# Replanned order, constant batches on GpSimd behind gates, and bound arithmetic on VectorE, in a graph and FFN layer

## The chip, the cores and the metric

One core of a Trainium2 chip runs the whole kernel. The metric is the device time of one execution in microseconds. Times of the parts come from one profiled execution.

## The reference

N = 3125 nodes of D = 256 features, E = 100,000 edges sorted by their target `dst`, each with a source and a relation (0 or 1).

```python
f = layernorm(x)
S = f[src]
msgs = where(rel == r, relu(relu(S @ W_rel[r].T + b_rel[r]) @ W_rel[r].T + b_rel[r]), ...)   # r = 0, 1
agg = segment_sum(msgs, dst, 3125)
i, f, g, o = split(agg @ W_ih.T + b_ih + b_hh, 4)
c = sigmoid(i) * tanh(g);  hn = sigmoid(o) * tanh(c)
x = x + relu(relu(hn @ W1.T + b1) @ W2.T + b2) @ W3.T + b3
n2 = layernorm(x);  w = n2 @ wr + br                 # one weight a node
sel = the 1561 nodes of largest w (ties to the lower index)
x = x + n2;  x[sel] += (gelu(n2[sel] @ w1 + b1) @ w2 + b2) * w[sel]
```

## The kernel before

The nodes lie in 25 blocks of 128, grouped in seven super-blocks (4, 4, 4, 4, 4, 3, 2 blocks). The messages depend on the source and the relation alone, so the **head** computes them once for each node and relation: for each super-block `s` a layer norm (`ln`, VectorE with a square root on ScalarE), transposes (`featT`), two products with the relation weights (`L1`, `L2`), and on VectorE `add_bias` and `low`, which with ScalarE write a high and a low fp16 half of each message to the tile `late` (`lows(s)` is this pair for all blocks of `s`). SyncE stores them to the table `message_table`. VectorE runs `lows(s)`, then `ln(s + 2)`, then one extra step; TensorE runs `L1(s)`, `featT(s + 1)`, `L2(s)`. TensorE waits for `ln`, and for at most three blocks of `add_bias` behind it.

The edges lie in 782 tiles of 128. The first 424 ("hot") are aggregated by counting: for each tile VectorE makes a mask of keys (`key`, L1723) and, for every four tiles, of rows (`rows`, L1732), TensorE multiplies them into banks (`count`, L1384), ScalarE evicts these counts (L1119), and `dense` (L1397) multiplies counts with the messages. The last 369 tiles ("cold") are gathered by GpSimd from the table, one indirect DMA a tile (L1046), into a ring of eight groups of four; TensorE sums a group with a mask (`visit`, L1416; a "chunk" is the part of a group that falls into one 128-node span), and frees it for GpSimd. GpSimd pauses behind every seventh group until the one before has landed. The tiles' places are predicted from statistics of the edges; **bounds** (`low_t`, `high_t`, `tile_low`, `width_t`) are written as 698 GpSimd memsets, and if an edge lies outside them, a general path, which otherwise costs nothing, takes over (`plan`).

Then, for each super-block: `aggT` (picks and adds the sums, L1274 and L1276), `gates`, `W1`, `W2`, `W3`, the residual, a second layer norm, `n2T`, and the FFN's `F1` (eight parts) and `down` (L1322). Eight rounds of `pick` find the weight of the last selected node; then the output is combined and stored. Gates, F1, `down` and the head are fp32.

**The order** of all of TensorE's work behind the head is a list, `steps_of`, made when the program is built by `schedule()`: it walks in planned time through the hot steps, the fixed steps and the chunks, with a cost of each step (`took`), the time that must lie before it (`ready`), and the landing of each group (`land`). VectorE's, ScalarE's and GpSimd's lists follow from it (`other_orders`). Each engine then runs its list in order, whatever the real times are. A chunk that has landed is put in when a ring slot is wanted or when nothing else can run.

In the head, GpSimd also has the rows of slots (`slot_row`, 47 operations, L987), the comparison of bounds (L989 to L996) and the additions of `b3` to the residual of super-blocks 2 to 6 (L1001); VectorE has `lows_of_tiles` (47 additions, L1530), the sum of the comparison (L1537, L1538) and `b3` for two super-blocks.

## Time and profile before

| | us |
|---|---|
| three runs | 749.86, 752.13, 757.51; median 752.13 |
| the profiled execution | 752.0 |
| its span, first to last instruction | 750.2 |

TensorE's mean granted clock in that execution was 0.956 of full speed. Times in the rows below are counted from the span's start. One fp32 matmul of the program shows as two instructions in the rows; a group "x24" of gates is twelve matmuls. A row of the timeline merges instructions of one kind that follow each other.

### The profile page before, as it was taken

How to read it: one execution, taken by the hardware profiler on the slowest of the kernel's cores; microseconds unless marked ns; L12 is line 12 of the kernel's file. 1: busy time of each engine (PE TensorE's matmuls, PEld its weight loads, DVE VectorE, ACT ScalarE, POOL GpSimd, SP SyncE). 2: the span in 40 equal slices, each digit the busy share in tenths (PEclk: the TensorE clock that was granted, in tenths of full speed). 3: DMA queues.
4: the chain of work that ended last, by engine and by line, in shares of the span. 5: the costliest groups of instructions: out<-in, count | busy, mean ns of one | idle time of the engine just before them, and what ended most of it. 6: DMA issues, size and time to landing. Idle time of an engine off the chain costs nothing.

```text
span 750.2 us, 9583 instructions
## 1 busy us (share of the span) xinstructions
PE 668.3 (89%) x3037; PEld 433.4 (58%) x3037; DVE 411.4 (55%) x1280; ACT 234.5 (31%) x403; POOL 445.9 (59%) x1301
## 2 busy tenths in 40 slices
PE   3978959689999999994857999999999999699986
PEld 2665638456666666653423666565665665377665
DVE  6764987898887988841215035143053244314475
ACT  1243234244333333300312333423414233032601
POOL 3567870376767676767777677647257677760000
PEclk9999979799999999997978999999999999799999
DMA  9300111333323333337333333313123332330005
GB/s 278 95 32 28 56 56 57 98 100 91 104 87 105 89 105 88 97 98 253 94 95 99 92 98 88 94 52 102 44 62 102 91 99 84 107 91 22 1 1 171
DMA packets 37881, 67.63 MB, mean 90 GB/s; under 512 B 7951, under 2 KB 25376, under 8 KB 37824
## 3 DMA queue, kind: packets, MB, share of 16 engines
q0 software_dynamic: 17712, 48.39, 22.0%
q1 hardware_dynamic: 19296, 17.77, 7.3%
q10 hardware_dynamic: 816, 0.79, 0.3%
q8 instruction: 26, 0.43, 0.2%
q14 instruction: 31, 0.25, 0.1%
HBM read 57.17 MB, written 9.75 MB: 89 GB/s over the span
## 4 chain that ended last, share of the span: by engine, by line
PE 75%; DVE 12%; POOL 6%; issue 3%; DMA 2%; ACT 2%; SPq 0%; DVEq 0%; POOLq 0%
PE BIG L1253 21%; PE SM L1397 12%; PE SM L1322 11%; PE AG L1416 10%; PE BIG L1384 6%; POOL ring L1046 5%; PE BIG L1212 4%; PE SM L1223 3%; PE BIG L1276 3%; PE AG L1223 2%; PE BIG L1193 2%; DVE half_b L1530 1%; DVE late L1514 1%; DVE ve L1484 1%; DMA ring<-message_table,rowT 1%
## 5 line engine op out<-in xcount | busy, mean ns | idle before, releaser
L1046 POOL DMA_INDIRECT ring<-message_table,rowT x369 | 366.3, 993 | 158.0 <-issue 106.1
L1416 PE MATMUL AG<-ring,onehot 128*128 128x512 f16 x369 | 95.3, 393 | 29.1 <-DMA ring<-message_table,rowT 25.2
L1322 PE MATMUL SM<-half_b,late 128*128 128x256 f32 x400 | 94.1, 383 | 1.5 <-DVEq L1598 0.8
L1322 PEld LDWEIGHTS SM<-half_b,late 128*128 128x128 f32 x400 | 74.5, 190 | 18.9 <-issue 5.7
L1253 PE MATMUL BIG<-fT,half_a 128*128 128x512 f32 (+1 forms) x192 | 81.4, 579 | 0.0
L1416 PEld LDWEIGHTS AG<-ring,onehot 128*128 128x128 f16 x369 | 41.5, 115 | 67.1 <-DMA ring<-message_table,rowT 16.6
L1253 PE MATMUL BIG<-half_b,half_a 128*128 128x512 f32 (+2 forms) x200 | 73.0, 521 | 0.5 <-ACT half_b L1135 0.5
L1397 PE MATMUL SM<-late,half_a 128*128 128x512 f16 x250 | 70.1, 381 | 0.7 <-ACT half_a L1119 0.7
L1767 DVE TENSOR_TENSOR onehot<-dst,iota_b 128x512 f16<-128x512 f16 (+3 forms) x115 | 45.0, 422 | 43.9 <-PE AG L1416 42.7
L1635 DVE TENSOR_TENSOR late<-late 128x1024 f32<-128x1024 f32 (+2 forms) x7 | 7.8, 1112 | 103.0 <-ACT late L1140 103.0
L1723 DVE TENSOR_SCALAR oh_key<-iota,lists 128x350 f16<-128x350 f16 (+8 forms) x228 | 58.8, 315 | 4.6 <-PE BIG L1384 4.0
L1384 PE MATMUL BIG<-oh_key,oh_row 128*128 128x150 f16 (+9 forms) x309 | 54.9, 270 | 7.2 <-DVE oh_row L1732 5.3
L1253 PEld LDWEIGHTS BIG<-fT,half_a 128*128 128x128 f32 x192 | 36.8, 193 | 40.2 <-issue 36.4
L1397 PE MATMUL SM<-late,half_b 128*128 128x512 f16 x200 | 58.8, 382 | 0.2 <-ACT half_a L1122 0.2
L1119 ACT ACTIVATE half_a<-BIG 128x500 f16<-128x500 f32 (+8 forms) x76 | 37.9, 515 | 67.6 <-PE BIG L1384 59.4
L1163 ACT ACTIVATE late<-BIG,fb 128x512 f32<-128x512 f32 (+2 forms) x56 | 35.6, 641 | 68.6 <-PE BIG L1253 68.6
L1253 PEld LDWEIGHTS BIG<-half_b,half_a 128*128 128x128 f32 x200 | 37.9, 190 | 31.7 <-issue 26.3
L1212 PE MATMUL BIG<-fT,WR 128*128 128x512 f32 (+2 forms) x112 | 48.4, 588 | 3.8 <-ACT ring L1103 3.0
L1732 DVE TENSOR_TENSOR oh_row<-row,iota 128x512 f16<-128x512 f16 x106 | 44.5, 422 | 11.4 <-PE BIG L1384 10.6
L1384 PEld LDWEIGHTS BIG<-oh_key,oh_row 128*128 128x128 f16 x309 | 31.7, 115 | 31.1 <-DVE oh_row L1732 6.6
L1119 ACT ACTIVATE half_b<-BIG 128x500 f16<-128x500 f32 (+8 forms) x62 | 29.8, 502 | 49.4 <-PE BIG L1384 41.4
L1140 ACT ACTIVATE late<-BIG,bg 128x512 f32<-128x512 f32 (+2 forms) x42 | 26.9, 641 | 42.9 <-PE BIG L1253 42.9
(194 smaller groups left out, 909.8 us busy)
## 6 DMA issues: line engine op xcount, KB each, us to landing
ring<-message_table,rowT POOLq DMA_INDIRECT x369, 2.8
message_table<-late SPq DMA_DIRECT2D x10, 512.0 KB, 3.6
out<-X SPq DMA_DIRECT2D x24, 128.0 KB
X<-in_x SPq DMA_DIRECT2D x4, 512.0 KB, 6.2
half_a<-in_f SPq DMA_DIRECT2D x1, 1024.0 KB, 7.7
half_b<-in_f SPq DMA_DIRECT2D x1, 1024.0 KB, 12.0
message_table<-late SPq DMA_DIRECT2D x2, 384.0 KB, 2.9
half_a<-in_w_ih_t SPq DMA_DIRECT2D x1, 768.0 KB, 4.3
```

Of the source, the lines that this page charges most:

```text
L1046: nc.gpsimd.indirect_dma_start(ring[:, to * W:(to + 1) * W], None, table, bass.IndirectOffsetOnAxis(ap=rowT[:, t:t + 1], axis=0)).then_inc ...
L1119: last = nc.scalar.activation(counts(lo // P)[:, lo % P:lo % P + mid - lo, :], b[:, 0:(mid - lo) * A].rearrange("p (n a) -> p n a", a=A), ...
L1212: last = nc.tensor.matmul(b[:, 0:n], WR[:, r, k, m * P:(m + 1) * P], fT[:, k, 0:n], start=(k == 0), stop=(k == KC - 1))
L1223: last = nc.tensor.matmul(b[:, r * D:(r + 1) * D], h1T[:, r, k, j * P:(j + 1) * P], WR[:, r, k, :], start=(k == 0), stop=(k == KC - 1))
L1253: last = nc.tensor.matmul(bank[:, 0:n], weight(k), data(k), start=(k == 0), stop=(k == depth - 1))
L1322: last = nc.tensor.matmul(bank, hidden_of(s)[:, c, j * P:(j + 1) * P], F2[:, c, :], start=(c == 0), stop=(c == HC - 1))
L1384: mm = nc.tensor.matmul(BIG[at[("big", "window", p)] % 4][:, (lo - at_slot) * A:(hi - at_slot) * A], rows[:, :, n % 4], key_slot(n)[:, (lo ...
L1397: mm = nc.tensor.matmul(bank[:, :], counts(k)[:, :, a], T[:, a, :], start=(a == 0), stop=(a == A - 1), skip_group_check=True)
L1416: mm = nc.tensor.matmul(AG[w % 2][:, :], hot[:, :, i], ring[:, to:to + W], start=(c == FIRST_OF[w] and i == lo), stop=(c == LAST_OF[w] and ...
L1723: made = nc.vector.tensor_scalar(key_slot(n)[:, 0:(hi - lo) * A], iota16[:, 0:(hi - lo) * A], keyT[:, t:t + 1], None, ALU.is_equal)
L1732: nc.vector.tensor_tensor(oh_row[:, to:to + 4 * P].rearrange("p (n t) -> p n t", t=4), row16[:, t:t + 4].unsqueeze(1).broadcast_to([P, P, 4]),
L1767: nc.vector.tensor_tensor(onehot[:, (c % OR) * 4 * P:(c % OR + 1) * 4 * P].rearrange("p (n t) -> p n t", t=4)[:, :, lo:hi], dst16[:, t + l ...
```

## The change

- `schedule()` gets other costs: `gates` 2.6 a block instead of 1.4, `W1`, `W3`, `F1` 0.43 instead of 0.24, `down` 0.43 instead of 0.24, `pick` 0.35 instead of 0.7; tiles, dense pieces and chunks a little less; `gates` to `W1` 3.1 instead of 5.0, `W3` to `n2T` 5.5 instead of 7.5; the first gather begins at 126.1 instead of 120.5 (counting stays at 118).
- The memsets of bounds keep their number and form eight batches. A batch waits for the end of `lows` of a super-block (even batches) or for the end of an `ln` (odd ones), instead of for one `add_bias` each. `tile_low` comes first.
- GpSimd computes nothing else ahead of the gathers. VectorE makes `slot_row` (`rows_of_slots`, behind `ln(3)`) and compares the bounds (`compare`, behind `ln(6)`); `b3` is added in VectorE's `gates` step.
- The first seven key masks are made behind `make_keys`, ahead of `lows(6)`, in the spare slots; `EARLY` is where the list of VectorE first has another step. TensorE waits for all `lows` ahead of the first dense piece and chunk and not ahead of counting. The slots' turn on TensorE moves from super-block 4 to 3.
- `aggT` starts its bank with its first part, and the matmul of zeros ahead of it goes.

```diff
     LOWS = segments(lowest, TW)
-    HIGHS = segments(lambda t: highest(t) - 1, TW)
+    HIGHS = segments(highest, TW)
     OFFSETS = segments(lambda t: OFFSET[t], TH)
-    WIDTHS = segments(lambda t: WIDTH[t] - 1, TH)
-    N_CONSTS = 13
+    WIDTHS = segments(lambda t: WIDTH[t], TH)
+    N_CONSTS = 12
     N_BOUNDS = len(LOWS) + len(HIGHS) + len(OFFSETS) + len(WIDTHS)
...
         far, keys_i, keys_i2 = dst_f[:, 0:TH], src_i, rel_i
-        over = prep[:, 6 * TW:8 * TW].rearrange("p (k t) -> p k t", k=2)
-        over_hot = prep[:, 3 * TW + TH:3 * TW + 3 * TH].rearrange("p (k t) -> p k t", k=2)
-        assert 3 * TH <= 2 * TW
         dst16 = sb("dst16", [P, TW - COLD], F16)
...
             i = t % KEYS_ON
-            return oh_key[:, i * 512:(i + 1) * 512] if i < KR else spare_keys[i - KR]
+            return spare_keys[i] if i < MORE_KEYS else oh_key[:, (i - MORE_KEYS) * 512:(i - MORE_KEYS + 1) * 512]
...
         ones16 = sb("ones16", [P, P], F16)
-        zeros16 = sb("zeros16", [P, P], F16)
         earlier = sb("earlier", [P, P], F16)
...
         bounds_set = sem("bounds_set")
-        lows_set = sem("lows_set")
-        capped = sem("capped")
-        biased = sem("biased")
-        over_ready = sem("over_ready")
         ident_ready = sem("ident_ready")
...
         def chosen_time(s):
-            return sum(hi - lo for o, _, lo, hi in CHOSEN if o == s) * KC * 4 / 2400
+            return sum(max(0.31, (hi - lo) * 4 / 2400) for o, _, lo, hi in CHOSEN if o == s) * KC
...
                     k = len(landed)
-                    begin = max(landed[-1] if landed else 120.5, waited[k - RQ] + 3.0 if k >= RQ else 0.0)
+                    begin = max(landed[-1] if landed else 126.1, waited[k - RQ] + 3.0 if k >= RQ else 0.0)
                     landed.append(begin + 1.25 * quad_tiles(k) + (3.0 if k in PAUSES else 0.0))
...
                 if kind == "tile":
-                    return sum(max(0.06, 0.02 + (hi - lo) * A / 2400) for _, lo, hi in HALVES[s])
+                    return sum(max(0.05, 0.005 + (hi - lo) * A / 2400) for _, lo, hi in HALVES[s])
                 if kind == "dense":
-                    return 0.218 * len(piece(s[1]))
+                    return 0.2145 * len(piece(s[1]))
                 if kind == "down":
-                    return 0.24 * len(down_parts(s[0])[s[2]])
+                    return 0.43 * len(down_parts(s[0])[s[2]])
                 if kind == "pick":
-                    return 0.7
+                    return 0.35
                 if kind == "ties":
...
                 nb = blocks(s[0] if kind == "F1" else s)
-                if kind == "aggT" and s < NH:
-                    return chosen_time(s) + 0.6 * len(spans_in(s)) + 0.5
-                return {"aggT": 0.3, "gates": 1.4, "W1": 0.24, "W2": 0.12, "W3": 0.24, "n2T": 0.25, "F1": 0.24}[kind] * nb
+                if kind == "aggT":
+                    return chosen_time(s) + 0.31 * KC * len(spans_in(s)) + 0.5
+                return {"gates": 2.6, "W1": 0.43, "W2": 0.22, "W3": 0.43, "n2T": 0.27, "F1": 0.43}[kind] * nb
...
                     return ends[("pick", s - 1)] + 2.5 if s else ends[("n2T", NS - 1)] + 2.5
-                before = {"gates": ("aggT", 1.6), "W1": ("gates", 5.0), "W2": ("W1", 1.1), "W3": ("W2", 1.1), "n2T": ("W3", 7.5)}
+                before = {"gates": ("aggT", 1.7), "W1": ("gates", 3.1), "W2": ("W1", 0.9), "W3": ("W2", 0.9), "n2T": ("W3", 5.5)}
                 if kind in before:
...
                 steps_of.append(("chunk", c))
-                now += 0.06 + 0.24 * (hi - lo)
+                now += 0.03 + 0.2145 * (hi - lo)
                 ends[("chunk", c)] = now
...
                     if kind == "tile":
-                        hot_at = max(hot_at, now - 5.0) + 0.27 + (TILES[s][2] - TILES[s][1]) * A * 0.00042
+                        hot_at = max(hot_at, now - 5.0) + 0.2 + (TILES[s][2] - TILES[s][1]) * A * 0.0005
                 elif can_fixed:
...
-        LISTS_AT, SLOTS_AT = 1, 4
+        LISTS_AT, SLOTS_AT = 1, 3
         BATCHES = 8
...
             full_at[("big",) + key] = sum(1 for k in big_items[:n + 1] if k[0] != "window")
+
+        EARLY = min(i for i, (kind, n) in enumerate(vector_steps) if kind not in ("key", "rows") or
+                    (kind == "key" and n >= MORE_KEYS))
...
             nc.gpsimd.memset(ones16[:, :], 1.0).then_inc(consts, 1)
-            nc.gpsimd.memset(zeros16[:, :], 0.0).then_inc(consts, 1)
...
                            allow_small_or_imprecise_dtypes=True).then_inc(consts, 1)
-            bounds = [(low_t, LOWS), (high_t, HIGHS), (width_t, WIDTHS), (tile_low, OFFSETS)]
+            bounds = [(tile_low, OFFSETS), (width_t, WIDTHS), (low_t, LOWS), (high_t, HIGHS)]
             bounds = [(t, lo, hi, v) for t, made in bounds for lo, hi, v in made]
             for i in range(BATCHES):
-                pool.wait_ge(summed, i + 1)
+                if i % 2 == 0:
+                    pool.wait_ge(lows_done, start_of(i // 2 + 1))
+                else:
+                    pool.wait_ge(feat_ready, i // 2 + 3)
                 for t, lo, hi, v in bounds[N_BOUNDS * i // BATCHES:N_BOUNDS * (i + 1) // BATCHES]:
                     nc.gpsimd.memset(t[:, lo:hi], float(v)).then_inc(bounds_set, 1)
-
-            pool.wait_ge(bounds_set, N_BOUNDS)
-            pool.wait_ge(consts, N_CONSTS)
-            pool.wait_ge(big_free, at[("big", "spread", 3)] + 1)
-            for j, (t, c, nodes) in enumerate(WINS):
-                first, k = min(a for a, _ in nodes), slots_of(nodes)
-                nc.gpsimd.tensor_scalar(slot_row[:, SLOT0[j]:SLOT0[j] + k], iota16[:, 0:k], tmin_b[:, c:c + 1], float(first),
-                                        ALU.add, ALU.add).then_inc(slots_ready, 1)
-            nc.gpsimd.tensor_tensor(over[:, 0, :], low_t, tmin_b, ALU.subtract).then_inc(over_ready, 1)
-            nc.gpsimd.tensor_tensor(over[:, 1, :], tmax_b, high_t, ALU.subtract).then_inc(over_ready, 1)
-            pool.wait_ge(lows_set, 1)
-            nc.gpsimd.tensor_tensor(over_hot[:, 0, :], tile_low, tmin_b[:, 0:TH], ALU.subtract).then_inc(over_ready, 1)
-            pool.wait_ge(capped, 1)
-            nc.gpsimd.tensor_tensor(far, far, tile_low, ALU.subtract).then_inc(capped, 1)
-            pool.wait_ge(capped, 2)
-            nc.gpsimd.tensor_tensor(over_hot[:, 1, :], far, width_t, ALU.subtract).then_inc(over_ready, 1)
-            pool.wait_ge(weights_in, 16 * N_LOADS)
-            for s in range(2, NS):
-                t, n = start_of(s), blocks(s)
-                pool.wait_ge(feat_ready, s + 1)
-                nc.gpsimd.tensor_tensor(X[:, t:t + n, :], X[:, t:t + n, :],
-                                        b3[:, :].unsqueeze(1).broadcast_to([P, n, D]), ALU.add).then_inc(biased, 1)
...
                 if s == SLOTS_AT:
-                    pe.wait_ge(slots_ready, NWIN)
+                    pe.wait_ge(slots_ready, 1)
                     b = big("slots")
...
                         b = big("aggT", s, c)
-                        nc.tensor.matmul(b[:, 0:n], zeros16[:, :], iota16[:, 0:n], start=True, stop=False, skip_group_check=True)
                         for i, (part, pick_of, lo, hi) in enumerate(parts):
-                            last = nc.tensor.matmul(b[:, lo:hi], part[:, c * P:(c + 1) * P], pick_of, start=False,
+                            last = nc.tensor.matmul(b[:, lo:hi], part[:, c * P:(c + 1) * P], pick_of, start=(i == 0),
                                                     stop=(i == len(parts) - 1), skip_group_check=True)
...
-            pe.wait_ge(lows_done, L2_ITEMS)
             pe.wait_ge(weights_in, 16 * N_LOADS)
...
+                if k == 0 and i == 0:
+                    pe.wait_ge(lows_done, L2_ITEMS)
                 if i == 0:
...
                 lo, hi = tiles_of(c)
+                if c == 0:
+                    pe.wait_ge(lows_done, L2_ITEMS)
                 if c == FIRST_OF[w] and w >= 2:
...
+            def rows_of_slots():
+                dve.wait_ge(big_free, at[("big", "spread", 3)] + 1)
+                for j, (t, c, nodes) in enumerate(WINS):
+                    first, k = min(a for a, _ in nodes), slots_of(nodes)
+                    last = nc.vector.tensor_scalar(slot_row[:, SLOT0[j]:SLOT0[j] + k], iota16[:, 0:k], tmin_b[:, c:c + 1],
+                                                   float(first), ALU.add, ALU.add)
+                last.then_inc(slots_ready, 1)
+
             def lows_of_tiles():
-                dve.wait_ge(bounds_set, N_BOUNDS)
-                dve.wait_ge(big_free, at[("big", "spread", 3)] + 1)
+                dve.wait_ge(bounds_set, len(OFFSETS))
                 for t, c, nodes in WINS:
                     m = len(nodes)
-                    last = nc.vector.tensor_scalar(tile_low[:, t:t + m], tile_low[:, t:t + m], tmin_b[:, c:c + 1], None, ALU.add)
-                last.then_inc(lows_set, 1)
-                nc.vector.tensor_scalar(far, tmax_b[:, 0:TH], float(HOT * P - 1), None, ALU.min).then_inc(capped, 1)
-
-            def sum_up():
-
-                dve.wait_ge(over_ready, 4)
-                nc.vector.tensor_reduce(tmm[:, 0, 0:1], over, AX.XY, ALU.max)
-                step(nc.vector.tensor_reduce(tmm[:, 0, 1:2], over_hot, AX.XY, ALU.max))
-                step(nc.vector.tensor_scalar(bad[:, :], tmm[:, 0, 0:1], tmm[:, 0, 1:2], 0.0, ALU.max, ALU.is_gt))
+                    nc.vector.tensor_scalar(tile_low[:, t:t + m], tile_low[:, t:t + m], tmin_b[:, c:c + 1], None, ALU.add)
+
+            def compare():
+                dve.wait_ge(bounds_set, N_BOUNDS)
+                nc.vector.tensor_tensor(low_t[:, 0:TH], low_t[:, 0:TH], tile_low, ALU.max)
+                step(nc.vector.scalar_tensor_tensor(far, tmax_b[:, 0:TH], float(HOT * P - 1), tile_low, ALU.min, ALU.subtract))
+                nc.vector.tensor_tensor(far, far, width_t, ALU.is_ge)
+                nc.vector.tensor_tensor(tmin_b, tmin_b, low_t, ALU.is_lt)
+                step(nc.vector.tensor_tensor(tmax_b, tmax_b, high_t, ALU.is_ge))
+                step(nc.vector.tensor_tensor(tmin_b, tmin_b, tmax_b, ALU.max))
+                step(nc.vector.tensor_tensor(tmin_b[:, 0:TH], tmin_b[:, 0:TH], far, ALU.max))
+                step(nc.vector.tensor_reduce(bad[:, :], tmin_b, AX.X, ALU.max))
                 nc.vector.tensor_scalar(away[:, 0:1], bad[:, :], FAR, float(-CENTER), ALU.mult, ALU.add)
...
-            def biases():
+            def key(n):
+                t, lo, hi = TILES[n]
+                if n == MORE_KEYS:
+                    dve.wait_ge(lows_done, NB)
+                if n >= KEYS_ON:
+                    dve.wait_ge(counted, ticked(n - KEYS_ON))
+                made = nc.vector.tensor_scalar(key_slot(n)[:, 0:(hi - lo) * A], iota16[:, 0:(hi - lo) * A], keyT[:, t:t + 1],
+                                               None, ALU.is_equal)
+                if n % 2 or n == TH - 1:
+                    made.then_inc(keys_made, 1)
+
+            def rows(q):
+                if q >= RR:
+                    dve.wait_ge(counted, ticked(4 * (q - RR) + 3))
+                t, to = TILES[4 * q][0], (q % RR) * 4 * P
+                nc.vector.tensor_tensor(oh_row[:, to:to + 4 * P].rearrange("p (n t) -> p n t", t=4),
+                                        row16[:, t:t + 4].unsqueeze(1).broadcast_to([P, P, 4]),
+                                        iota16[:, 0:4 * P].rearrange("p (n t) -> p n t", t=4), ALU.is_equal).then_inc(rows_made, 1)
+
+            def bias_sum():
                 dve.wait_ge(weights_in, 16 * N_LOADS)
                 nc.vector.tensor_tensor(bg[:, :], bi[:, :], bh[:, :], ALU.add).then_inc(bias_ready, 1)
-                for s in range(2):
-                    t, n = start_of(s), blocks(s)
-                    nc.vector.tensor_tensor(X[:, t:t + n, :], X[:, t:t + n, :],
-                                            b3[:, :].unsqueeze(1).broadcast_to([P, n, D]), ALU.add)
...
                 lows(s)
+                if s == LISTS_AT:
+                    bias_sum()
                 if s + 2 < NS:
                     ln(s + 2)
-                if s == 1:
-                    biases()
-                elif s == 2:
+                if s == LISTS_AT:
+                    rows_of_slots()
+                elif s == LISTS_AT + 1:
                     lows_of_tiles()
-                elif s == 3:
+                elif s == LISTS_AT + 2:
                     split_rows()
-                elif s == 4:
-                    sum_up()
-                elif s == 5:
+                elif s == LISTS_AT + 3:
+                    compare()
+                elif s == NS - 2:
                     make_keys()
+                    dve.wait_ge(big_free, at[("big", "slots")] + 1)
+                    for kind, n in vector_steps[:EARLY]:
+                        if kind == "key":
+                            key(n)
+                        elif kind == "rows":
+                            rows(n)
             def residual(s):
-                if s >= 2:
-                    dve.wait_ge(biased, s - 1)
                 for q in range(pairs(s)):
...
                 n = blocks(s) * P
+                t, k = start_of(s), blocks(s)
+                nc.vector.tensor_tensor(X[:, t:t + k, :], X[:, t:t + k, :],
+                                        b3[:, :].unsqueeze(1).broadcast_to([P, k, D]), ALU.add)
                 dve.wait_ge(big_free, at[("big", "gate", s, 3)] + 1)
...
-            def key(n):
...
-            def rows(q):
...
-
             def dense_sum(k):
...
-            for kind, s in vector_steps:
+            for kind, s in vector_steps[EARLY:]:
                 if kind == "key":
...
                 elif kind == "rows":

```

## Rows read from the trace of the kernel before

**Rows 1.** The page, part 1: busy us (share of the span) and instructions of each engine.
```profile
PE 668.3 (89%) x3037; PEld 433.4 (58%) x3037; DVE 411.4 (55%) x1280; ACT 234.5 (31%) x403; POOL 445.9 (59%) x1301
```

**Rows 2.** Windows by stage: length, each engine's busy us (instructions), granted clock, DMA share, GB/s.
```profile
61.00:107.00 46.00, 37.24 (x130) 23.29 (x129) 35.01 (x94) 14.28 (x27) 38.84 (x56) 0.91 0.14 46
...
160.00:320.00 160.00, 159.43 (x985) 105.93 (x985) 136.56 (x504) 59.39 (x126) 116.20 (x164) 1.00 0.33 96
320.00:349.00 29.00, 18.69 (x90) 10.99 (x89) 11.20 (x41) 1.76 (x3) 20.71 (x34) 0.90 0.59 194
349.00:400.00 51.00, 35.61 (x135) 20.72 (x134) 13.79 (x38) 10.41 (x14) 37.88 (x50) 0.83 0.34 98
400.00:640.00 240.00, 239.10 (x897) 145.70 (x896) 78.59 (x202) 80.95 (x111) 155.90 (x228) 0.99 0.29 85
640.00:690.00 50.00, 42.85 (x185) 29.73 (x183) 17.43 (x44) 10.10 (x17) 27.17 (x40) 0.90 0.26 77
```

**Rows 3.** Timeline, 26 to 60 us: start, us, engine, line, what [idle before, releaser].
```profile
26.73 12.48 POOL L980 MEMSET half_a<- 128x83 f32 x328 [19.49 <-DVE oh_key L1509]
...
35.41 4.53 DVE L1484 TENSOR_SCALAR ve<-mv 128x4 f32<-128x4 f32 x1
...
41.86 1.28 PE L1193 MATMUL BIG<-ident,agg_ring 128*128 128x128 f32 x8 [3.88 <-DVE agg_ring L1488]
...
55.83 3.28 DVE L1484 TENSOR_SCALAR ve<-mv 128x4 f32<-128x4 f32 x1
```

**Rows 4.** Timeline, 82 to 107 us.
```profile
82.67 10.38 DVE L1530 TENSOR_SCALAR half_b<-half_b,ring 128x28 f32<-128x28 f32 x47
...
96.78 8.29 POOL L1001 TENSOR_TENSOR X<-X,b 128x1024 f32<-128x1024 f32 x3
...
97.89 4.98 DVE L1514 SCALAR_TENSOR_TENSOR late<-oh_key,late 128x512 f16<-128x512 f32 x2
...
106.69 1.54 PE L1193 MATMUL BIG<-ident,agg_ring 128*128 128x128 f32 x6 [8.76 <-DVE agg_ring L1488]
```

**Rows 5.** Windows of line L1530 alone: length, VectorE's busy us (instructions), clock, DMA.
```profile
83.00:84.00 1.00, 1.00 (x9) 1.00 0.00 0
```

**Rows 6.** Timeline, 121 to 143 us: the end of the head.
```profile
121.05 2.01 DVE L1537 TENSOR_REDUCE tmm<-ring 128x1 f32<-128x1792 f32 x1
...
138.66 1.34 DVE L1723 TENSOR_SCALAR oh_key<-iota,lists 128x100 f16<-128x100 f16 x8 [0.32 <-DVE late L1514]
...
140.38 0.32 PE L1384 MATMUL BIG<-oh_key,oh_row 128*128 128x100 f16 x3 [4.16 <-DVE oh_row L1732]
...
142.13 1.68 POOL L1046 DMA_INDIRECT ring<-message_table,rowT  x1 [19.64 <-DMA message_table<-late]
```

**Rows 7.** Timeline of TensorE, 347 to 436 us.
```profile
347.64 1.87 PE L1416 MATMUL AG<-ring,onehot 128*128 128x512 f16 x4 [9.64 <-DMA ring<-message_table,rowT]
...
383.31 1.90 PE L1416 MATMUL AG<-ring,onehot 128*128 128x512 f16 x4 [6.25 <-DMA ring<-message_table,rowT]
...
417.79 2.05 PE L1276 MATMUL BIG<-oh_row,more_sums 128*128 128x64 f32 x14
...
425.36 10.46 PE L1253 MATMUL BIG<-half_b,half_a 128*128 128x512 f32 x24
```

**Rows 8.** The ring's waits (us, times, longest), the last gather, and the last aggT.
```profile
POOL ring L1046 <- PE AG L1416: 28.6, 11, 11.6
...
676.25 0.95 POOL L1046 DMA_INDIRECT ring<-message_table,rowT  x1 [0.30 <-issue]
...
689.42 0.28 PE L1274 MATMUL BIG<-iota,zeros 128*128 128x256 f16 x1 [0.79 <-DVE WR L1776]
```

**Rows 9.** Groups by form, line L1630: busy us, mean ns.
```profile
L1630 DVE TENSOR_TENSOR X<-X,half_b 128x1024 f32<-128x1024 f32 x5 | 6.1, 1225 | 0.2
```

**Rows 10.** The waits of VectorE's gates step: us in total, times, longest.
```profile
DVE late L1635 <- ACT late L1140: 103.0, 7, 28.8
```

**Rows 11.** The ring's waits between 500 and 560 us.
```profile
POOL ring L1046 <- PE AG L1416: 16.2, 2, 11.6
```

15 lines of the change are left out of this document (removed).

## The prediction

> **What bounds the kernel now.** I read the page's busy times first [rows 1]: TensorE works 668 of 750 us, no other engine 60%. So the question is where TensorE stands still or runs slowly. The windows by stage answer it [rows 2]. From 160 to 320 us (counting tiles and dense work) it is busy 159.4 of 160, from 400 to 640 it is busy 239 of 240; nothing that shortens a wait of another engine pays there. The idle time lies in four places: the head before 140 us, 320 to 400 us (10.3 and 15.4 us idle, at a granted clock of 0.90 and 0.83), 640 to 690 (7.2 us idle), and the tail after the last gather. The timeline then tells what it waits for in each.
>
> In the head, TensorE's feature transposes wait for VectorE's layer norm. The small `ve` operation, on four columns, took 4.53 and 3.28 us while GpSimd ran memsets, 328 of them in 12.5 us, and the transposes started at 41.9, 3.9 us late [rows 3]. Later VectorE's 47 additions of tile bounds (10.4 us) and its last `low` operations (4.98 us for two, beside GpSimd's 1,024-column additions) make the transposes of super-block 5 late by 8.8 us [rows 4]. Counting starts at 140.4 us, the first gather at 142.1 [rows 6].
>
> After the counting, TensorE's order is fixed at build time, and it stands in it for chunks whose gathers have not landed: 9.6 us at 347.6, 6.3 us at 383.3, with W1 of super-block 0 queued behind them [rows 7]. That is an order made with wrong times: the gates of four blocks took 10.5 us [rows 7] and were planned at 5.6 (1.4 a block). GpSimd's gathers are the second chain: from 142.1 to 677.2, of which 28.6 us were spent waiting for TensorE to free the ring [rows 6, 8]. Its own pace needs 677.2 - 142.1 - 28.6 = 506.5 us. aggT of the last super-block starts at 689.4, 12 us after the last gather [rows 8], and 60.8 us of tail follow to 750.2.
>
> **The change, part by part.** I walk through four places, each as the time by which its end comes earlier.
>
> *Head, memsets.* There are 698 bound memsets in eight batches, at 0.035 to 0.038 us each 3.1 us a batch. Before, the L2 blocks of one super-block let four batches go together. Now one starts when `lows(s)` is done and one when `ln` is. The first kind runs beside the bn_stats (some 2.2 us) and holds `ve` for the rest, about 1 us. I take the row's behaviour, a batch that is not let go until it ends. The first transposes move from 41.9 to 38.4 (3.5 us), the second gap shrinks from 3.0 to under 1 (2.2 us). Had `ve` only waited for one memset, these batches would cost the changed kernel nothing.
>
> The Trainium skill says something else of this: in "SBUF — State Buffer", section "Who interferes with whom", the pair of ports that VectorE and GpSimd share is a lock held for one whole instruction. By that `ve` would wait for one memset of 0.04 us and not for 328; the trace does not agree (4.53 us). By the rule the new gates would be free and the head some 4 us shorter than I work out.
>
> *Head, GpSimd's work given to VectorE.* GpSimd's 47 slot rows (26.7 us), its bound comparisons and all its bias additions go. VectorE gets the 47 slot rows. No row shows that operation on VectorE; the nearest is the addition of bounds, nine a us while GpSimd ran long operations beside it [rows 5] and 0.22 us each on the whole [rows 4], so 5 to 10 us, and a batch of memsets may hold them 3 us more. I take 5.5 plus 3 us. They lie after ln(3), where VectorE was idle for 8 us waiting for L2: nothing on the path. The 47 bound additions shrink from 10.4 to some 5.5 but start behind a memset batch (3.1 us): they end some 5 us later than lows(3) could begin. VectorE makes that up at 1.37 us a block against TensorE's 1.73, and what is left after ln(5) is a wait of some 2 us where there were 8.8. With the clock after the gap (0.91 in 61 to 107 us, [rows 2], about 4 us lost) this gives 6 to 10 us, and I take 8.
>
> *Head, comparison.* `compare` is five operations over 896 and four over 424 columns. An addition over 1,024 columns takes 1.23 us [rows 9], so 896 take 1.07; with the short ones 7.1 us, against 3.7 for the reductions removed (2.0 the first, [rows 6]). It lies before lows(5) and pushes them by about 3 us; TensorE has four banks and doesn't notice, but the last `low` does, since make_keys and seven key masks (7 x 0.17 us, [rows 6]) come before lows(6). It ends 14 us earlier, not 16. Counting then needs one key and one row mask instead of eight and one: 1.3 us. Only keys fit ahead, the first row mask sorts behind the eighth key, so this part is worth no more. The bias sum (0.16 us) moves nowhere that matters.
>
> Sum of the head: 3.5 + 2.2 + 8 + 1.3 = 15 us for the counting (125.1), 14 for the first gather (128.2). Bounds 8 (the batches hold more than `ve`) and 19 (they hold nothing).
>
> *Residual biases.* Seven additions of up to 1.23 us enter VectorE's gates step, ahead of its wait for the gates' sigmoids. VectorE idles 103 us over seven such waits [rows 10], so they hide; without that cover they would cost 7.8 us. Behind them on VectorE stand masks for the gathered chunks, made 5 us ahead.
>
> *Hot part.* TensorE does the same matmuls; it moves by 15 us. The new plan has it at some 182 us (tiles 57, dense 96, chunks 28), the chip took 196 (140.4 to 336.8): the plan will ask for a few chunks too few rather than too many, so it does not wait for gathers. Before, the plan had 218.
>
> *From the end of counting to aggT of super-block 1.* It took 337 to 417.8 us [rows 7]. A full instruction of four blocks takes 0.43 us there (24 in 10.5 us, [rows 7]), so gates 10.3 and F1, of 32, 13.8; with some 8 for aggT(0) and 5 for W1 to n2T, together 37; the waits between them that no order removes come to some 15 (the plan's 1.6, 3.1, 0.9, 0.9, 5.5, 1.4 and 2.0 at the start). The order can put 9 us of landed chunks into them. 55 us in place of 81, so 24 to 26 us, of which some 7 are the clock (0.83 to 0.90 granted for 80 us, [rows 2]). The zero matmuls removed are 14 x 0.21 to 0.4 us: 4 us in all. aggT(1) then starts at 320 + 55 = 375 to 378.
>
> *From there to the last aggT.* TensorE took 271.6 us (417.8 to 689.4), with 8 us idle. Unchanged it would arrive at 378 + 271.6 - 3 = 646; without its idle time 639. GpSimd arrives at 128.2 + 506.5 = 634.7, plus 2.8 for landing, a visit and the close: 639 if TensorE never stops it. Both chains come out within 7 us, so neither is free of the other. I add some 5 us for gathers still held up: 645.
>
> *Tail.* gates(6), W1 to W3, the rounds of picks and the last down products hang on each other in the same order: 60.8 us, unchanged.
>
> The span is 645 + 60.8 = 706; the profiled execution was 752.0 for a span of 750.2, so 708 us. The median of the runs, 752.13, is the same as that execution's time. That is 44 us or 5.9% less: 15 head, 25 behind the counting, 4 zeros and the rest of the idle time.
>
> **The rivals.** *Only the head counts.* The new order moves the 25 us of waiting elsewhere: TensorE leaves early, then runs ahead of the gathers and waits for them in 540 to 640 us. GpSimd's 28.6 us of waiting remain, it ends at 128 + 535 = 663, the last aggT is at 675, and the time is 737. For it speaks that 400 to 640 us is full now, partly because gathers were ahead; against it that 16.2 of the 28.6 us fell between 500 and 560 [rows 11], where TensorE was far behind its plan, and it would be 40 us earlier there.
>
> *Gathers run free.* The order visits chunks as they land and TensorE keeps its pace: 639 + 60.8 + 1.8 = 701.
>
> *The gathers are starved by the order.* Should the new order put the fixed work, whose planned cost nearly doubled, ahead of chunks, GpSimd stands at a full ring. Every us beyond the 10 or so between the chains lengthens the end one for one. It decides when its waits grow from 28.6 to about 75 us: 128 + 506 + 75 + 12 + 62.6 = 784, slower by 4%; break-even is 43. Against it: the planner visits a chunk as soon as the ring is within three groups of full.
>
> *The head does not shrink*, because memset batches hold the bound additions and key splitting fully, and every `low` as well: 8 us instead of 15, so 715.
>
> **How the numbers follow.** Forecast (701 to 715, three of the cases overlap in it) 0.65; free gathers within it; only the head counts, 716 to 742: 0.25; better than 698: 0.05; starved gathers 0.05, of which 0.02 within 1% of before and 0.03 slower. 1%, 7.5 us, is about what this kernel's runs can tell from no change. Low end 697, high end 733: this leaves out the stronger half of the second case and the rarer ones. Faster 0.94, same 0.03, slower 0.03.
>
> **What would show it.** Right: `ve` near 1 us, no wait over 3 us of TensorE before counting, which starts near 125; the first gather near 128; aggT(1) before 380; waits of the ring on TensorE under 15 us; the last gather by 645. Wrong: a wait of TensorE for gathers over 5 us between 320 and 380, a last gather after 655, or slot rows that keep VectorE from lows(2). The likeliest error is in the interplay after 400 us, which I sum and do not follow chunk by chunk.

## The result and the profile after

The changed kernel takes 716.61 us (median of four runs, 715.27 to 719.81), beside 751.0 for the kernel before on the same chip: a ratio of 0.9536, 95% interval 0.9466 to 0.9606. The forecast was 708, with a range of 697 to 733. The profiled execution has a span of 715.0 us.

The forecast's own band for the favoured case ended at 715; the measured time lies inside the range, 1.6 us above that band.

The page, part 1, and windows by stage (length, busy us and instructions of TensorE, its weight loads, VectorE, ScalarE, GpSimd, then granted clock, DMA share, GB/s):

```profile
PE 658.6 (92%) x3023; PEld 427.4 (60%) x3023; DVE 415.4 (58%) x1336; ACT 234.0 (33%) x403; POOL 407.6 (57%) x1243
```

```profile
146.00:306.00 160.00, 158.57 (x981) 105.58 (x980) 134.53 (x503) 59.47 (x125) 116.43 (x164) 1.00 0.33 96
...
320.00:380.00 60.00, 46.37 (x148) 23.38 (x147) 19.35 (x46) 17.02 (x23) 42.72 (x65) 0.86 0.38 117
380.00:620.00 240.00, 233.40 (x896) 143.78 (x895) 88.75 (x220) 74.49 (x102) 176.09 (x246) 0.99 0.33 96
620.00:655.00 35.00, 34.37 (x153) 25.82 (x151) 10.58 (x28) 10.01 (x16) 15.41 (x27) 0.95 0.21 61
655.00:715.00 60.00, 48.60 (x240) 36.30 (x238) 34.31 (x121) 18.98 (x34) 0.00 (x0) 0.98 0.16 54
```

Beside [rows 2]: the full stage behind the start of counting is the same work at the same speed, 13.6 us idle remain in 320 to 380, and 6.6 appear in 380 to 620, where TensorE was full before.

Five marks carry the whole gain. Counting starts at 122.4 instead of 140.4, the first gather at 126.1 instead of 142.1 [rows 6]. aggT of super-block 1 starts at 382.1 instead of 417.8 [rows 7], the last gather at 640.6 instead of 676.3, the last aggT at 654.6 instead of 689.4 [rows 8]. The tail from there is 60.4 us, 60.8 before. So 18.0 us come from the head, 17.7 between the start of counting and aggT(1), and 0.8 are given back from there to the last aggT.

The head, timeline of the changed kernel (start, us):

```profile
33.57 2.96 POOL L977 MEMSET half_b<- 128x12 f32 x87 [26.49 <-DVE late L1491]
...
35.68 0.88 DVE L1461 TENSOR_SCALAR ve<-mv 128x4 f32<-128x4 f32 x1
...
38.48 1.09 PE L1168 MATMUL BIG<-ident,agg_ring 128*128 128x128 f32 x8 [0.22 <-DVE agg_ring L1465]
...
50.84 0.87 DVE L1461 TENSOR_SCALAR ve<-mv 128x4 f32<-128x4 f32 x1
...
74.34 8.30 DVE L1514 TENSOR_SCALAR half_b<-half_b,ring 128x28 f32<-128x28 f32 x47
74.47 1.09 PE L1168 MATMUL BIG<-ident,agg_ring 128*128 128x128 f32 x8
...
92.01 4.62 POOL L977 MEMSET half_a<- 128x11 f32 x88 [0.84 <-DVE agg_ring L1465]
92.15 0.82 PE L1168 MATMUL BIG<-ident,agg_ring 128*128 128x128 f32 x6
...
122.40 0.44 PE L1357 MATMUL BIG<-half_b,oh_row 128*128 128x100 f16 x3 [3.07 <-DVE oh_row L1561]
...
126.10 1.17 POOL L1021 DMA_INDIRECT ring<-message_table,rowT  x1 [29.47 <-DMA message_table<-late]
```

The two `ve` of [rows 3], 4.53 and 3.28 us, take 0.88 and 0.87: each ends with its batch of 87. The transposes that started at 41.9 start at 38.5. Those of super-block 5, which came at 106.7 with 8.8 us of waiting [rows 4], come at 92.2 with none.

### The profile page after: what moved, and what is told of

It is laid out like the page before. It is cut to its first block, busy times and chain, and to the rows that moved or that the text cites. A ratio compares the mean times of both kernels' runs of the same rounds, so it can differ in the third digit from the quotient of the medians.

```text
span 715.0 us, 9546 instructions
## 1 busy us (share of the span) xinstructions
PE 658.6 (92%) x3023; PEld 427.4 (60%) x3023; DVE 415.4 (58%) x1336; ACT 234.0 (33%) x403; POOL 407.6 (57%) x1243
## 4 chain that ended last, share of the span: by engine, by line
PE 50%; POOL 22%; DVE 11%; issue 9%; DMA 4%; ACT 2%; POOLq 0%; SPq 0%; DVEq 0%
POOL ring L1021 22%; PE BIG L1228 14%; PE SM L1372 8%; PE SM L1296 7%; PE AG L1393 5%; PE BIG L1357 5%; DMA ring<-message_table,rowT 3%; PE BIG L1187 3%; PE AG L1198 2%; PE SM L1198 2%; PE BIG L1250 2%; PE BIG L1168 1%; DVE half_b L1514 1%; DVE oh_key L1552 1%; DVE oh_key L1486 1%
## 5 line engine op out<-in xcount | busy, mean ns | idle before, releaser
L1393 PE MATMUL AG<-ring,onehot 128*128 128x512 f16 x369 | 94.4, 385 | 19.9 <-DMA ring<-message_table,rowT 19.5
L1228 PE MATMUL BIG<-fT,half_a 128*128 128x512 f32 (+1 forms) x192 | 84.8, 590 | 0.8 <-issue 0.7
L1758 DVE TENSOR_TENSOR onehot<-dst,iota_b 128x512 f16<-128x512 f16 (+3 forms) x115 | 44.8, 423 | 34.4 <-PE AG L1393 33.5
L1552 DVE TENSOR_SCALAR oh_key<-iota,lists 128x150 f16<-128x150 f16 (+8 forms) x224 | 56.9, 308 | 4.3 <-PE BIG L1357 3.8
L1645 DVE TENSOR_TENSOR late<-late 128x1024 f32<-128x1024 f32 (+2 forms) x7 | 7.8, 1111 | 87.2 <-ACT late L1115 87.2
L1228 PEld LDWEIGHTS BIG<-half_b,half_a 128*128 128x128 f32 x200 | 37.8, 190 | 31.6 <-issue 26.3
L1357 PE MATMUL BIG<-oh_key,oh_row 128*128 128x250 f16 (+8 forms) x299 | 51.5, 263 | 2.0 <-DVE oh_key L1552 0.8
L1561 DVE TENSOR_TENSOR oh_row<-row,iota 128x512 f16<-128x512 f16 x106 | 44.2, 418 | 13.5 <-PE BIG L1357 12.9
L977 POOL MEMSET half_b<- 128x1 f32 (+2 forms) x370 | 12.9, 99 | 50.5 <-DVE late L1491 46.6
```

The source lines that it names most:

```text
L1228: last = nc.tensor.matmul(bank[:, 0:n], weight(k), data(k), start=(k == 0), stop=(k == depth - 1))
L1357: mm = nc.tensor.matmul(BIG[at[("big", "window", p)] % 4][:, (lo - at_slot) * A:(hi - at_slot) * A], rows[:, :, n % 4], key_slot(n)[:, (lo ...
L1393: mm = nc.tensor.matmul(AG[w % 2][:, :], hot[:, :, i], ring[:, to:to + W], start=(c == FIRST_OF[w] and i == lo), stop=(c == LAST_OF[w] and ...
L1552: made = nc.vector.tensor_scalar(key_slot(n)[:, 0:(hi - lo) * A], iota16[:, 0:(hi - lo) * A], keyT[:, t:t + 1], None, ALU.is_equal)
L1561: nc.vector.tensor_tensor(oh_row[:, to:to + 4 * P].rearrange("p (n t) -> p n t", t=4), row16[:, t:t + 4].unsqueeze(1).broadcast_to([P, P, 4]),
L1758: nc.vector.tensor_tensor(onehot[:, (c % OR) * 4 * P:(c % OR + 1) * 4 * P].rearrange("p (n t) -> p n t", t=4)[:, :, lo:hi], dst16[:, t + l ...
```

## The experiments

Each is the changed kernel with one part edited, but for p1_plan_only, which is the kernel before with new planned times. Ratios are to the kernel before, run beside it on the same chip; it took 751.7 us beside p1 to p4, 754.2 beside g1, g2, v1 and h1, and 752.3 beside the others.

| run | median us | ratio, 95% interval |
|---|---|---|
| the changed kernel | 716.61 | 0.9536 (0.9466 to 0.9606) |
| p1_plan_only | 732.79 | 0.9724 (0.9676 to 0.9771) |
| p2_old_plan | 735.16 | 0.9782 (0.9731 to 0.9833) |
| p3_old_hot | 731.34 | 0.9703 (0.9658 to 0.9749) |
| p4_old_fixed | 733.85 | 0.9741 (0.9697 to 0.9785) |
| p5_old_start | 726.82 | 0.9669 (0.9603 to 0.9735) |
| v2_real_landing | 716.42 | 0.9519 (0.9479 to 0.9558) |
| g1_slow_gathers | 730.88 | 0.9715 (0.9658 to 0.9773) |
| g2_short_pause | 719.11 | 0.9533 (0.9472 to 0.9593) |
| v1_last_first | 720.0 | 0.956 (0.9503 to 0.9618) |
| h1_bias_pool | 721.82 | 0.9583 (0.9529 to 0.9636) |
| h2_batches_early | 721.08 | 0.9571 (0.9528 to 0.9614) |
| h3_no_early_keys | 717.63, one run | |

An interval is some 4 us wide to either side. So g2, v1, v2 and h3 cannot be told from the changed kernel by their time, and h1 and h2 hardly; for these the marks of the trace are the evidence. At a line of 2% p2_old_plan stays unclear, since its interval reaches 0.9833; that it is faster than the kernel before is clear.

### Head and order apart

p1_plan_only puts the new planned times into the kernel before, and nothing else. p2_old_plan puts the old ones into the changed kernel.

```diff
-                return {"aggT": 0.3, "gates": 1.4, "W1": 0.24, "W2": 0.12, "W3": 0.24, "n2T": 0.25, "F1": 0.24}[kind] * nb
+                return {"gates": 2.6, "W1": 0.43, "W2": 0.22, "W3": 0.43, "n2T": 0.27, "F1": 0.43}[kind] * nb
...
```

> The kernel before with the new planned times alone (no other part of the change). If the reorder works by itself: the head stays (counting near 140 us, first gather near 142), aggT of super-block 1 comes some 65 us after the end of counting instead of 81, and the gathers' waits for the ring fall from 28.6 to under 8 us, so the last gather is near 142 + 510 = 652 and the time near 652 + 14 + 62 = 728 to 734. Rival, that the head's 16 to 18 us are all that counts: 745 to 752.

> The changed kernel with the old planned times (head and all the rest as changed). If head and order add up: counting near 122, first gather near 126, but waits of TensorE near 10 and 6 us for gathers behind the counting, ring waits of 20 to 30 us, last gather near 126 + 535 = 661, time 733 to 738. Rival, that an early head cures the order as well: 717 to 722.

Both came as expected in time and in waits. The order alone gives 18.9 us (751.7 to 732.8), the rest alone 16.5 (751.7 to 735.2), together 35.4, and the whole change gave 34.4: they add up, and neither cures the other's loss. The ring's waits for TensorE tell the order: 28.6 us before, 25.6 with the old plan and the new head, 3.4 with the new plan and the old head, 3.7 in the changed kernel.

### Which planned time matters

p3_old_hot takes back the planned start of the gathers, the pace of counting and the cost of tiles; p5_old_start the first of these alone; p4_old_fixed the costs and gaps of the fixed steps.

```diff
-                    begin = max(landed[-1] if landed else 126.1, waited[k - RQ] + 3.0 if k >= RQ else 0.0)
+                    begin = max(landed[-1] if landed else 120.5, waited[k - RQ] + 3.0 if k >= RQ else 0.0)
```

> The changed kernel where only the planned start of the gathers (120.5), the pace of counting and the cost of tiles are the old ones. If TensorE's long wait behind the counting comes of these (too many chunks placed in and just behind the counting): a wait of 5 to 10 us for gathers appears before the first aggT, counting's end stays; since the gathers bound the end, only up to 5 us of it reaches the time: 717 to 724. Rival, that these do nothing: 715 to 718 and no wait.

> The changed kernel with one number of the plan old: the first gather planned 2.5 us behind the counting's start instead of 8.1 (on the chip 3.7 us, plus 8 us until the first group has landed). With this, the pace of counting and the cost of tiles old, it was 731. If the start is the cause: gathers' waits before the first aggT of 4 to 8 us again and 724 to 732. If the pace is: 715 to 720.

> The changed kernel where only the costs of aggT, gates, W1 to W3, n2T, F1, down and the waits between them are the old, too small ones. If these starve the ring: it waits 20 to 30 us for TensorE between 380 and 560 us and the time is 732 to 742. Rival, that the start and the pace of counting matter more: ring waits under 10 us and 716 to 722.

Each half taken back costs 15 to 17 us (12.5 and 15.4 by the ratios), nearly the whole of the order's gain. Seen from the old plan, one half put right brings 1 to 4 us (735.2 to 733.9 and 731.3; 3 and 6 by the ratios), and both together 18.6: the two do not add up. The mechanism differs. aggT(1) and the last gather of p3_old_hot, from the timeline:

```profile
406.12 2.05 PE L1250 MATMUL BIG<-oh_row,more_sums 128*128 128x64 f32 x14
...
643.33 0.95 POOL L1021 DMA_INDIRECT ring<-message_table,rowT  x1 [0.30 <-issue]
```

and of p4_old_fixed:

```profile
372.54 2.05 PE L1250 MATMUL BIG<-oh_row,more_sums 128*128 128x64 f32 x14
...
657.61 0.95 POOL L1021 DMA_INDIRECT ring<-message_table,rowT  x1 [0.30 <-issue]
```

With the fixed steps planned too short, TensorE does them early (aggT(1) at 372.5, 10 us ahead of the changed kernel), the ring fills, GpSimd waits 23.2 us for it, 20.5 of them between 380 and 560 us, and the last gather comes 17 us later. (The edit puts back short costs and long gaps together; which of the two does it was not tested.) With counting planned too slow and the gathers too early, the gathers never wait (1.2 us), but TensorE stands 22.4 us for chunks between 290 and 400, aggT(1) comes 24 us later, and though the last gather is in time, the last aggT is at about 672: TensorE's own chain is late. The start alone is some 10 of the 15 us (aggT(1) at 393.8, last aggT at 664.8). Its time was as expected, the place was not: no wait for gathers stands before the first aggT, and 17.0 us of them behind it. My expectation for p3_old_hot, 717 to 724, rested on the gathers alone bounding the end; that fell.

### Which chain bounds the end

g1_slow_gathers makes each of GpSimd's 13 pauses 1.1 us longer, with 44 memsets of one column instead of 12 of four; g2_short_pause takes eleven of the twelve memsets out.

```diff
-        pause_out = sb("pause_out", [P, 12, 4])
+        pause_out = sb("pause_out", [P, 44, 1])
...
-                    for i in range(12):
+                    for i in range(44):
                         last = nc.gpsimd.memset(pause_out[:, i, :], 0.0)
```

> The changed kernel with 32 more memsets in each of GpSimd's 13 pauses, 1.1 us each, so the gathers end 15 us later. If the gathers bound the end (22% of the chain are theirs): last gather near 655, time up by 8 to 15 us, 725 to 731. Rival, that TensorE's chain bounds it and has the gathers' time to spare: under 4 us, 716 to 721.

> The changed kernel with one memset instead of twelve in each pause: gathers end up to 5 us earlier. If the gathers bound the end: 711 to 714, as the last chunks and the waits in 320 to 380 come earlier. If both chains are equally long (10 us of TensorE's work are left behind the last chunk): no change, 715 to 718.

Slower gathers pass through in full: last gather 13.3 us later (653.9), last aggT 13.3 us later (667.8), time 14 us up. The chain that ended last, followed back in the changed kernel, agrees: from 511 to 644 us it runs through the gathers. The shorter pause did not test the other side, and its 719.1 us lie outside both ranges that I gave. One pause of the changed kernel and the same of g2_short_pause:

```profile
202.51 0.45 POOL L1013 MEMSET pause_out<- 128x4 f32 x12 [1.83 <-DMA ring<-message_table,rowT]
203.23 1.20 POOL L1021 DMA_INDIRECT ring<-message_table,rowT  x1 [0.27 <-POOL pause_out L1013]
...
204.20 0.10 POOL L1013 MEMSET pause_out<- 128x4 f32 x1 [1.85 <-DMA ring<-message_table,rowT]
204.90 1.20 POOL L1021 DMA_INDIRECT ring<-message_table,rowT  x1 [0.60 <-POOL pause_out L1013]
```

The memsets are 0.35 us shorter, and the wait for their end is 0.33 us longer, so the pause keeps its length. The waits for landed groups even grew, from 27.3 to 31.6 us in 13 pauses, and the last gather came at 644.9. So slower gathers lengthen the time one for one; whether faster ones shorten it stays open.

v2_real_landing gives the plan the mean pace of the gathers that the changed kernel's trace shows.

```diff
-                    landed.append(begin + 1.25 * quad_tiles(k) + (3.0 if k in PAUSES else 0.0))
+                    landed.append(begin + 1.2875 * quad_tiles(k) + (2.8 if k in PAUSES else 0.0))
```

> The changed kernel with the landings planned at the pace that its trace shows (1.2875 us a gather instead of 1.25, 2.8 us a pause instead of 3.0: the last group 11 us later in the plan). In the changed kernel TensorE stands four times for gathers ahead of W1, W2, W3 and n2T of super-block 0 (3.1, 2.1, 1.9, 2.2 and 3.7 us). If that is the plan's fault: waits for gathers fall from 19.5 to under 10 us, aggT of super-block 1 starts 5 to 10 us earlier than 382, time 705 to 713. If the waits are those of the chain itself, with chunks as filling: no change, 714 to 719.

No change in time; the waits for gathers are 19.1 us, 19.5 in the changed kernel, and aggT(1) starts at 380.7. This fits the rival's number, but the traces do not bear out its reason. The chunks do hold the chain up. VectorE in the changed kernel, the last operation ahead of W1:

```profile
337.61 1.23 DVE L1648 TENSOR_TENSOR late<-late 128x1024 f32<-128x1024 f32 x1 [3.15 <-ACT late L1118]
```

W1's input is ready at 338.8, and W1 starts at 342.5, behind a chunk that waits for its gather until 341.6. W2 is held for 2.7 us in the same way, W3 for 2.0, n2T for 3.7: 12 us in all. In v2_real_landing W2's input is ready at 342.4 and W2 starts at 350.0, behind two chunks. The waits moved and did not go.

Nor was the plan right there. schedule() of v2_real_landing lets the 38th group of gathers land at 335.8 (331.1 in the changed kernel); on the chip TensorE waits for it until 344.6 (341.6). A mean pace misses one long pause:

```profile
315.19 0.51 SPq L933 DMA_DIRECT2D half_a<-in_f  x1
...
323.00 0.45 POOL L1013 MEMSET pause_out<- 128x4 f32 x12 [5.21 <-DMA ring<-message_table,rowT]
```

SyncE loads the weights of the gates and of the FFN then (2.9 MB), the DMA engines are full from 318 to 324 us (385 GB/s; 93 from 306 to 312), and this pause waits 5.2 us where the other twelve wait 1.8 to 1.9. In the kernel before and in p2_old_plan no pause falls beside these loads (longest wait 2.6 and 1.9); in every run with the new order or most of it one does (5.1 to 6.6). No run moves the loads, so their part is argued. What a plan with the landings as they are would bring stays untested.

v1_last_first moves the last aggT ahead of the last down products of super-block 4.

```diff
...
-            fixed.append([("n2T", y)] + quarters(y - 1, 3, 2, 3))
-            fixed.append([("aggT", z), ("gates", z)] + hidden(y, 0, 2))
...
+            fixed.append([("aggT", z), ("n2T", y), ("gates", z)] + quarters(y - 1, 2, 0, 1, 2, 3))
...
```

> The changed kernel with aggT and n2T of the last two super-blocks ahead of the last down products of super-block 4, which go between the last gates, W1 and W2. In the changed kernel 10 us of TensorE's work (W3, 32 down instructions, transposes) lies between the last chunk at 644 and the last aggT at 654.6. If these 10 us delay the end and the tail has room (48.6 busy of 60 us): last aggT near 647, tail longer by some 3 to 6 us, time 709 to 713. Rival, that TensorE's work is conserved and only moves: 715 to 718.

The last chunks and what follows, timeline of TensorE, changed kernel:

```profile
643.93 0.41 PE L1393 MATMUL AG<-ring,onehot 128*128 128x512 f16 x1 [0.41 <-DMA ring<-message_table,rowT]
...
646.90 5.45 PE L1296 MATMUL SM<-half_b,late 128*128 128x256 f32 x24 [0.22 <-DVEq L1605]
...
654.57 0.29 PE L1250 MATMUL BIG<-ident,agg_ring 128*128 128x17 f32 x2
...
675.63 0.34 PE L1306 MATMUL AG<-oh_key,ones 128*128 128x80 f16 x5
```

and v1_last_first:

```profile
646.40 0.41 PE L1393 MATMUL AG<-ring,onehot 128*128 128x512 f16 x1 [0.63 <-DMA ring<-message_table,rowT]
...
648.99 0.29 PE L1250 MATMUL BIG<-ident,agg_ring 128*128 128x17 f32 x2
...
653.47 0.87 PE L1168 MATMUL BIG<-ident,half_b 128*128 128x128 f32 x6 [2.54 <-DVE half_b L1619]
...
677.90 0.34 PE L1306 MATMUL AG<-oh_key,ones 128*128 128x80 f16 x5
```

From the last chunk to the last aggT it takes 2.6 us instead of 10.6, as meant, but to the first round of picks 31.5 instead of 31.7: the products moved stand ahead of the picks as well, and a wait of 2.5 us for the layer norm is new. TensorE is busy for 29.0 of these 31.5 us, and for 30.0 of 31.7 in the changed kernel: the work is conserved, and what the tail lacks is TensorE time before the picks. The tail grew by 7.9 us, where I had expected 3 to 6, and the time, 720.0, is above both ranges that I gave.

### The head taken apart

h1_bias_pool gives the additions of `b3` for super-blocks 2 to 6 back to GpSimd:

```diff
+            for s in range(2, NS):
+                t, n = start_of(s), blocks(s)
+                pool.wait_ge(feat_ready, s + 1)
+                nc.gpsimd.tensor_tensor(X[:, t:t + n, :], X[:, t:t + n, :],
+                                        b3[:, :].unsqueeze(1).broadcast_to([P, n, D]), ALU.add).then_inc(biased, 1)
```

> The changed kernel with b3 added on GpSimd in the head for super-blocks 2 to 6, as before (11.9 us on GpSimd, now between 96 and 109 us, beside lows(4), ln(6) and the comparison). If these additions delay VectorE's work with two SBUF inputs as in the kernel before (4.98 us for two low operations): counting 3 to 8 us later, 125 to 130, and 719 to 725. Rival, that only the memset batches hold VectorE: counting at 122 to 123 and 715 to 718.

Its timeline:

```profile
96.25 10.10 POOL L983 TENSOR_TENSOR X<-X,b 128x1024 f32<-128x1024 f32 x4
96.29 0.69 DVE L1493 TENSOR_TENSOR oh_key<-SM,onehot 128x512 f32<-128x512 f32 x1 [0.96 <-PE SM L1205]
96.90 2.26 DVE L1498 SCALAR_TENSOR_TENSOR late<-oh_key,late 128x512 f16<-128x512 f32 x1
...
109.45 1.12 PE L1175 MATMUL BIG<-ident,agg_ring 128*128 128x128 f32 x4 [4.58 <-DVE agg_ring L1472]
...
128.26 0.32 PE L1364 MATMUL BIG<-half_b,oh_row 128*128 128x100 f16 x3 [3.08 <-DVE oh_row L1568]
```

`low` reads two tensors from SBUF and takes 2.2 us instead of 0.68 beside GpSimd's additions; `add_bias`, which reads one of its two from PSUM, keeps its 0.69. The transposes wait 4.6 us, the four take 1.12 us instead of 0.60, and counting starts 5.9 us later, as expected. This agrees with the Trainium skill, "SBUF — State Buffer", "Who interferes with whom": a VectorE instruction with two SBUF inputs contends with a GpSimd instruction that reads SBUF.

h2_batches_early lets the batches go by one `add_bias` each:

```diff
-                if i % 2 == 0:
-                    pool.wait_ge(lows_done, start_of(i // 2 + 1))
-                else:
-                    pool.wait_ge(feat_ready, i // 2 + 3)
+                pool.wait_ge(summed, i + 1)
```

> The changed kernel with the batches of memsets let go by one add_bias each, as before. If a run of memsets holds VectorE's operation until it ends: the small operation of ln(2) takes some 4.5 us again, that of ln(3) 3 us, TensorE's first two gaps return (about 4 and 3 us), less the stalls of the later batches; counting at 125 to 129 and 719 to 724. Rival, that the lock is let go after each memset: counting at 121 to 123, 714 to 718.

Its memsets and the two `ve`, timelines of GpSimd and of VectorE:

```profile
27.07 11.91 POOL L974 MEMSET half_b<- 128x12 f32 x349 [19.99 <-DVE oh_key L1483]
...
45.25 12.53 POOL L974 MEMSET half_a<- 128x17 f32 x328
```

```profile
35.75 3.26 DVE L1458 TENSOR_SCALAR ve<-mv 128x4 f32<-128x4 f32 x1
...
53.29 1.80 DVE L1458 TENSOR_SCALAR ve<-mv 128x4 f32<-128x4 f32 x1
```

The first `ve` is held until the memsets end at 39.0, the second is not: it ends at 55.1, the memsets at 57.8. Counting starts at 124.5, 2.1 us late. That is just under the 125 to 129 that I expected; in the eight other runs with the changed head it lies between 121.3 and 122.8.

h3_no_early_keys makes the seven masks after the last `low`:

```diff
-                    for kind, n in vector_steps[:EARLY]:
+                    for kind, n in []:
...
-            for kind, s in vector_steps[EARLY:]:
+            for kind, s in vector_steps:
```

> The changed kernel with the first seven key masks made behind the last low operation, as before. Seven masks at 0.16 us, less the time by which they push lows(6): counting starts 0 to 1.5 us later than 122.4 (the first at 122.5 to 124), the first gather up to 0.8 us earlier, since the last store no longer waits for the masks. No time outside 712 to 722.

Counting starts at 123.9, 1.5 us later, the first gather at 126.05, the same. From the one to the other it takes 2.2 us instead of 3.7, and this difference does not hang on how early the head is in a run. The time, 717.63, cannot be told from the changed kernel's.

## Why the prediction was right, point by point

One of its signs failed: aggT(1) was to start before 380 us and started at 382.1. By number alone 716.6 falls where the forecast had "only the head counts" (716 to 742); by its marks it is the favoured case, with chunks that hold TensorE up. The span came out 9 us longer than the 706 of the sum. Counting starts 2.7 us earlier than forecast and the hot part is 1.2 us shorter, which hides part of two terms that were too small, 10 us before aggT(1) and 3.5 behind it.

*Memset batches.* Right in mechanism, and right in size as far as the gaps go: `ve` 0.9 us, transposes at 38.5 (forecast 38.4), the second gap 0.7 us instead of 3.0. h2_batches_early undoes it in part: `ve` 3.3 and 1.8 us instead of 4.5 and 3.3, and 2.1 us at the start of counting, where the forecast had 5.7 for both gaps. Its memsets come in another order than those of the kernel before, so it does not show what the full effect is worth.

*GpSimd's work on VectorE.* I took 5.5 + 3 us for the slot rows, and they take 8.8 us (53.7 to 62.5):

```profile
L1506 DVE TENSOR_SCALAR half_a<-iota,ring x47: 125/221/3012, 53.7 to 62.3; 128x22 f32<-128x22 f16 x5, 128x23 f32<-128x23 f16 x5, 128x21 f32<-128x21 f16 x4, 128x37 f32<-128x37 f16 x3
```

One of 47 lasts 3.0 us, held by its batch, and they end when the first L2 block is ready (its `add_bias` starts at 62.4, 2.0 us behind the start of L2, as in the super-blocks before). The bound additions took 8.3 (forecast 8.6). The wait for ln(5) was forecast at 2 us and was 0; key splitting was not held (1.9 us in all). This makes most of the 18.0 us instead of 15 for counting and of the 16.0 instead of 14 for the gathers. The comparison took 7.0 us where I had 7.1, but with four operations over 896 columns, not five. TensorE did notice it: ScalarE, held behind it, lets L2 of the last super-block wait 1.5 us.

*Early keys.* 1.3 us forecast, 1.5 measured, no earlier row mask.

*Hot part.* From the start of counting to the first aggT's parts 194.8 us, forecast 196. I had read the new plan wrong: schedule() puts them 197.7 us behind the start of counting (118.0 to 315.7), not 182. The forecast took the chip's 196 and was not harmed by it.

*From counting to aggT(1).* The mis-sized term: 55 us forecast, 65 measured (317.2 to 382.1), 81 before. (The parts named, 37 and 15, make 52 and not 55.) I put the chunks into the chain's gaps at no cost. TensorE of the changed kernel there:

```profile
341.57 1.05 PE L1393 MATMUL AG<-ring,onehot 128*128 128x512 f16 x4 [3.07 <-DMA ring<-message_table,rowT]
342.46 1.88 PE L1228 MATMUL BIG<-late,W 128*128 128x512 f32 x4
346.46 1.53 PE L1393 MATMUL AG<-ring,onehot 128*128 128x512 f16 x4 [2.12 <-DMA ring<-message_table,rowT]
...
361.56 1.90 PE L1393 MATMUL AG<-ring,onehot 128*128 128x512 f16 x4 [3.65 <-DMA ring<-message_table,rowT]
...
382.13 2.05 PE L1250 MATMUL BIG<-oh_row,more_sums 128*128 128x64 f32 x14
```

Chunks stand ahead of each step of the chain and wait for their gathers, 12.9 us in five waits, and the steps are held by 12 us, as shown above. The clock was 0.86 of full, and F1(0) took 16.4 us where the forecast has 13.8 at full speed, 2.6 us of the loss. The plan itself has 52.8 us here. It lets the 38th group land 10.5 us too early, and aggT(1) starts 13.6 us behind the plan's 368.5. A better mean pace (v2_real_landing) does not remove the waits; a plan with the long pause in it was not tried. The same loads bear on the wait of 9.6 us in [rows 7], which the forecast put down to the order alone: they start at 337.1 there, and the DMA engines are full until 348.

*From there to the last aggT.* Forecast 269 us or less, measured 272.4. Chunks visited in that stretch, windows of their line alone, before and after:

```profile
417.80:689.00 271.20, 45.06 (x185) 20.95 (x185) 0.98 0.29 84
```

```profile
382.00:654.00 272.00, 50.31 (x201) 22.29 (x201) 0.99 0.31 91
```

TensorE is 36 us earlier, the gathers 16, so 16 tiles more are left to visit (5.3 us), and that ate the 4 us of zeros removed. The idle time was not saved: 7.2 us of 272.5, 8.0 before. The ring's waits fell to 3.7 us (forecast under 15), yet the gathers needed 511.7 us of their own, forecast 506.5: their pauses wait 27.3 us for landings, 24.7 before, and the long one makes up that difference. The last gather ends at 641.5, within the forecast, but the last aggT follows 13.1 us later, 10 us behind the 645 of the sum. The sum gave 4 us to what lies behind the last gather, though [rows 8] show 12, and both slower rivals reckon with 12. The term is TensorE's: W3 and down products behind the last chunk. v1_last_first takes them out of that place, and they come back in the tail.

*Residual biases, tail.* The tail takes 60.4 us against 60.8. VectorE still idles 87.2 us (103 before) ahead of the seven gates steps, so the additions are hidden, as forecast; no run takes them out by themselves.

*The rivals.* "Only the head counts" (737) is refuted: the order alone brings 18.9 us in p1_plan_only, and the ring's waits are 3.7 us and not 28.6. "Gathers run free" (701) is true of the ring, but TensorE did not keep its pace up to aggT(1), and its work behind the last chunk is not in that sum. The head shrank by 18 us, not 8. Starved gathers is a real mechanism: p4_old_fixed shows it (23.2 us of ring waits, 17 us of time), in the direction opposite to the one I argued. It comes from fixed steps planned too short, not too long.

## What to carry to other kernels

When a list of work is fixed by planned times, errors on either side cost: steps planned too short starve the producer of the ring, transfers planned too early stop the consumer, and either alone took back 12 to 17 us of 19. So put both sides right before judging the result. Then lay the planned landings beside the measured ones, step by step where the consumer waits and not on the mean: here one pause beside a bulk load was 3.4 us longer than the rest. Where a head engine's small operation gates a long chain, look at which neighbour runs long beside it, and give many short memsets their place behind the operation that must not wait.
